# Delta stage of a decoder block: the 16x16 block inversion cut into five pieces in VectorE's queue, the decay scans given four slots

## The reference, cut to what matters

```
S = S * exp(g_t)
v_eff = (v_t - k_t S) * beta_t
S = S + k_t^T v_eff
o_t = q_t S
```

## Time and profile before

| | us |
|---|---|
| median of 3 runs | 1939.47 |
| lowest, highest run | 1939.33, 1945.62 |
| the profiled execution, its own time | 1945.92 |
| its span (first to last instruction) | 1944.0 |
| outside the span | 1.9 |

### The profile page before, as it was taken

One profiled execution on the slowest core, in us unless ns is written; L12 is line 12 of the kernel. 1 busy time (PEld: TensorE's weight loads), 2 busy tenths in 40 slices (PEclk: granted clock), 3 DMA queues, 4 the chain that ended last, 5 costly groups with the idle time before them and its releaser, 6 DMA issues. The chain is left out here.

```text
span 1944.0 us, 31429 instructions
## 1 busy us (share of the span) xinstructions
PE 1594.6 (82%) x10849; PEld 1132.2 (58%) x10849; DVE 1147.0 (59%) x2425; ACT 820.8 (42%) x1745; POOL 597.3 (31%) x547
## 2 busy tenths in 40 slices
PE   5898972379999999857589999999747999999980
PEld 3444442368888878743247776676634666666650
DVE  4898993355676666423235677777753554554545
ACT  3777771024444434423345555555312333333324
POOL 0222224222233330010023355454542333333330
PEclk9898985678899888978699999999868999999995
DMA  2232325434334543203611222310321111111117
GB/s 85 85 140 86 141 86 151 131 88 132 102 92 136 134 121 91 61 21 123 208 51 40 92 72 67 116 34 23 135 94 31 45 47 47 45 47 48 44 39 262
DMA packets 180536, 174.48 MB, mean 90 GB/s; under 512 B 87352, under 2 KB 139116, under 8 KB 180268
## 3 DMA queue, kind: packets, MB, share of 16 engines
q1 hardware_dynamic: 165771, 145.49, 24.0%
q0 software_dynamic: 10400, 22.95, 3.6%
q10 hardware_dynamic: 4224, 4.19, 0.6%
HBM read 112.54 MB, written 60.04 MB: 89 GB/s over the span
## 5 line engine op out<-in xcount | busy, mean ns | idle before, releaser
L520 DVE SCALAR_TENSOR_TENSOR conv_y<-conv_in,taps,conv_y 128x512 f32<-128x512 f32 x192 | 165.3, 875 | 19.2 <-ACT conv_y L391 14.7
L2204 POOL DMA_INDIRECT y<-o,idx x71 | 83.4, 1175 | 242.0 <-DVE o L2347 234.0
L2283 ACT ACTIVATE xsT<-pX 128x256 f32<-128x256 f32 x71 | 27.3, 384 | 303.3 <-PE pX L2228 303.3
L1647 PE MATMUL xQ<-late,last 128*128 128x512 f32 x256 | 127.2, 620 | 16.5 <-ACT late L1803 7.8
L2239 PE MATMUL pG<-w_gu,xsT 128*128 x284 | 135.5, 600 | 1.2 <-issue 0.6
L2260 PE MATMUL pD<-late,hT 128*128 x568 | 134.2, 379 | 0.0
L2239 PE MATMUL pU<-w_gu,xsT 128*128 x284 | 134.1, 594 | 0.0
L316 PE MATMUL ps_j<-xnT,w_qkv 128*128 128x512 f32 x256 | 131.2, 649 | 0.0
L1613 POOL TENSOR_TENSOR sc<-sc,den 128x1232 f32<-128x1232 f32 x32 | 72.0, 2249 | 174.6 <-DVE den L2029 174.5
L2260 PEld LDWEIGHTS pD<-late,hT 128*128 128x128 f32 x568 | 102.5, 190 | 11.0
L2343 DVE TENSOR_TENSOR o<-pD,late 128x256 f32<-128x256 f32 x71 | 30.1, 424 | 121.1 <-PE pD L2260 121.1
(11 more groups left out here) (316 smaller groups left out, 3818.6 us busy)
## 6 DMA issues: line engine op xcount, KB each, us to landing
qkvg<-tok SPq DMA_DIRECT2D x8, 2048.0 KB, 6.6
qkvg<-gate SPq DMA_DIRECT2D x8, 1024.0 KB, 8.8
step<-step SPq DMA_DIRECT2D x32, 256.0 KB, 5.5
qk<-qkvg SPq DMA_DIRECT2D x32, 256.0 KB, 6.9
vb<-qkvg SPq DMA_DIRECT2D x32, 256.0 KB
gt<-qkvg SPq DMA_DIRECT2D x32, 256.0 KB
y<-y SPq DMA_DIRECT2D x16, 512.0 KB
xin<-in_x SPq DMA_DIRECT2D x11, 512.0 KB, 4.0
```

Source lines behind the costliest of these rows:

```text
L520: y = nc.vector.scalar_tensor_tensor(conv_y[m % 4][:], conv_in[b][:, m, k:k + BT], taps[:, m, k:k + 1], conv_y[m % 4][:], ALU.mult, ALU.add)
L1647: mm = pe.matmul(Q[:], w_q[:, c, j * P:(j + 1) * P], x1T[:, c, :], start=c == 0, stop=c == KD - 1)
L2204: nc.gpsimd.indirect_dma_start(out=s["y"].rearrange("t p d -> (t p) d"), out_offset=bass.IndirectOffsetOnAxis(ap=idx[j % 8][:, 0:1], axis= ...
```

## The change

`run` gets a fourth function, `rest`, which it calls last in each slot, behind the tails. Only DVE passes one. The four scans go from `new` in slots 3 and 5 (two each) to `rest` in slots 2, 3, 4 and 5 (one each). The inversion is cut into pieces, also in `rest`: `first_blocks` in slot 9, merges 2 and 4 in slot 10, the first half of merge 8 (`upper_left`) in slot 11, its second half (`lower_right`) and `last_blocks` in slot 12. The arithmetic and the number of instructions are the same; the other engines' queues are unchanged. The core of the diff:

```diff
-        def run(new, ready, tail):
+        def run(new, ready, tail, rest=None):
...
                             tail((f - 4 * b) % SLOTS, n, n % 2, b)
+                    if rest and 0 <= c + 2 < CHUNKS:
+                        rest(f, c + 2)
...
-            def merged_blocks(m):
...
+            def upper_left(m):
+                n, w, v, wide = block_views(m)
+                link(each(v, m, corner(X16, m, 0, 0), corner(N16, m, 0, 1)))
+                link(nc.vector.tensor_reduce(W16[:, 0:w], V16[:, 0:w * m].rearrange("p (w j) -> p w j", j=m), AX_X,
+                                             ALU.add))
+
+            def lower_right(m):
+                n, w, v, wide = block_views(m)
+                link(each(v, m, wide, corner(X16, m, 1, 1)))
                 link(nc.vector.tensor_reduce(corner(X16, m, 0, 1), v, AX_X, ALU.add, negate=True))
...
             def new(f, c, par):
-                if f in (3, 5):
-                    for b in (FIRST, SECOND)[f // 5]:
-                        decays(c, b)
                 if f == 6:
...
+            def rest(f, c):
+                if f in (2, 3, 4, 5):
+                    decays(c, f - 2)
+                if f == 9:
+                    first_blocks(c)
                 if f == 10:
-                    first_blocks(c)
-                    merged_blocks(2)
-                    merged_blocks(4)
+                    for m in (2, 4):
+                        upper_left(m)
+                        lower_right(m)
                 if f == 11:
-                    merged_blocks(8)
+                    upper_left(8)
+                if f == 12:
+                    lower_right(8)
                     last_blocks()
...
-            run(new, ready, tail)
+            run(new, ready, tail, rest)
```

More of the change, by code:

```diff
@@ L1086, in first_blocks, with block_views, each @@
                 link(nc.vector.tensor_tensor(X16[:, 0:LANE], X16[:, 0:LANE], con[:, C_L1:C_L1 + LANE], ALU.add))
-            def merged_blocks(m):
+            def block_views(m):
                 n = B0 // (2 * m)
-                shape, w = [P, m, m, m], n * m * m
+                w = n * m * m
                 v = V16[:, 0:w * m].rearrange("p (n i k j) -> p n i k j", n=n, i=m, k=m)
[L1092 to L1101, removed]
+                return n, w, v, W16[:, 0:w].rearrange("p (n i k) -> p n i k", n=n, i=m)
+            def each(v, m, left, right):
+                shape = [P, m, m, m]
+                for q in range(B0 // (2 * m)):
+                    last = nc.vector.tensor_tensor(
+                        v[:, q], left[:, q].unsqueeze(2).broadcast_to(shape),
+                        right[:, q].rearrange("p j k -> p k j").unsqueeze(1).broadcast_to(shape), ALU.mult)
+                return last
+            def upper_left(m):
+                n, w, v, wide = block_views(m)
+                link(each(v, m, corner(X16, m, 0, 0), corner(N16, m, 0, 1)))
                 link(nc.vector.tensor_reduce(W16[:, 0:w], V16[:, 0:w * m].rearrange("p (w j) -> p w j", j=m), AX_X,
                                              ALU.add))
-                link(each(wide, corner(X16, m, 1, 1)))
+            def lower_right(m):
+                n, w, v, wide = block_views(m)
+                link(each(v, m, wide, corner(X16, m, 1, 1)))
                 link(nc.vector.tensor_reduce(corner(X16, m, 0, 1), v, AX_X, ALU.add, negate=True))
```

## The result

| | before | changed |
|---|---|---|
| median of 7 runs, us | 1942.26 (1938.01 to 1947.89) | 1955.79 (1938.91 to 1961.17) |
| ratio, 95% interval | | 1.0058 (1.0033 to 1.0083) |
| profiled execution, us (span) | 1945.92 (1944.0) | 1953.18 (1951.3) |

The changed kernel is slower by 0.6%, some 11 us; 1941 was forecast, and the measured median lies above the range's 1951. Repeated beside the experiments it gave 1.0046 (1.0026 to 1.0066). The loss lies in the delta stage: DVE's last statistics of it come at 864.3 us of the span before and at 870.8 after, and what follows takes 1079.7 and 1080.5 us. Of the 7.3 us between these two spans 3.6 are not the change but luck of the clock.

The account below looks back on a forecast made before the run. PE was taken to set the pace, busy 53.9 of about 58 us a step. Terms 0.8 + 6 x 0.04 + 1.8 - 1.2 = +1.6 us, added to the median 1939.47, gave 1941; range 1933 to 1951.

Parts of the forecast that it names:

- the scans' half: DVE's slots 2 to 6: the instruction list is the same before and after, so spreading the scans does nothing by itself.
- ACT, not the inversion, holds the gating of b2: Gating of b2: ACT's root is late by itself, so PE's 2.39 us stall stays; DVE's shift there +0.04 us a step.
- the +0.8 forecast: Step -1: the Y round falls behind the wait for N, moving z6 copies and `base_done` back +0.8 us, once.
- 4.5: `base_done` moves 4.5 us later in the step, and the DMAs behind it on SP shift by as much.
- The term of the scans: PE's stall on the Z round shrinks as POOL waits for loads: -0.2 us a step, -1.2 us in six.
- the y6 wait at 0.3 us a step: y6 on PE waits for the first z6 copy: 0.3 us a step, bounds 0.2 and 0.5, +1.8 us in six.
- the late loads at nothing: SP's loads behind `base_done` shift by 4.5 us, but b1's keys still land before PE wants them: cost 0.
- steady machine: Stages of a full step: about 58 us each, PE busy 53.9 of them and setting the pace.
- a margin of 1.5 us: Keys of b1: landing 9.77 us behind T's issue, from step 0, leaves 1.5 us where it was 5.6.
- Rival B: Loads land over 11.3 us behind T's issue; PE waits at L839 in five steps: 7.5 to 15 us slower, chance 0.15.
- Rival A: The low clock stretch behind PE's stall shrinks by luck of position: up to 15.4 us faster, chance 0.18 in all.
- Full and part: Low clock shrinking in all six steps, -15.4 us, chance 0.05; in one to three, -2.6 to -7.7 us, chance 0.13.

Follow-up runs that it names:

- e1: Kernel before with only the four scans moved to their new slots, the inversion left in `new`: ratio 1.0006 (0.9989 to 1.0024).
- e5: Changed kernel with the next chunk's scores loads of batches 0 to 2 issued ahead of the inverses, against the kernel before: ratio 0.9932.
- e8: Kernel before with the scores loads of batches 0 to 2 issued ahead of the inverses, DVE's queue untouched: ratio 0.9900 (0.9874 to 0.9925).
- e11: The kernel of e5 again, on the chip of e10, against the kernel before: ratio 0.9950 (0.9933 to 0.9968).
- e10: Changed kernel with `lower_right(8)` and `last_blocks` behind the z6 copies and the loads early as in e5, against the kernel before: ratio 0.9882.
- e4: Kernel before with SP sending the inverses only after DVE's z6 copies, DVE's queue untouched: ratio 1.0042 (1.0028 to 1.0057).
- e2: Kernel before with only merge 8's second half and `last_blocks` moved behind the targets of b3: ratio 1.0051 (1.0031 to 1.0072).

## Why the prediction was wrong

Right, by its own steps: the scans' half does nothing. ACT, not the inversion, holds the gating of b2, and the stall stays 2.39 us in six steps. In step -1 the time from the first use of N to the z6 copies grew from 7.77 us (395.45 to 403.22) to 8.58 (394.59 to 403.17), +0.81 for the +0.8 forecast. `base_done` moved by 4.4 us for 4.5. N was in use 3.05 us after its issue (619.10 to 622.15), the very figure of the earlier trace rows; `first_blocks` waited 0.71 us for it and PE lost nothing. The term of the scans had the right sign: PE's waits on Z in front of L841 are 2.5 us in four steps where they were 4.6 in five, for the 1.2 us forecast, though two of the four are still 0.95 us.

The step that failed is the one that put the y6 wait at 0.3 us a step and the late loads at nothing. Together they were +1.8 us in the sum. In the changed kernel's trace they are 3.6 us at y6 and a wait of 2.52 us for keys with a low clock behind it, and the change as a whole costs 9 to 11 us. Both were sized in a long step, and the kernel doesn't only have long steps. The "steady machine" of the first paragraph was one execution; e1 shows the same queue at 54.35 us a step.

- The wait at y6. From gating to the copies DVE's work has a fixed length (4.03 us). PE's work in between, the transposes and updates b3, is shorter at full clock (L933 1.16 us in place of 1.91). So the half clock hid four fifths of the wait: 0.30 us at half, 1.38 at full. With the loads early, e5 lies 0.3% above e8, and e11 lies 0.5% above e8 and 0.7% above e10.
- The loads. I had a margin of 1.5 us: landing 9.77 us behind T's issue, need 11.3 us behind it. In the step with the wait PE was ready for the keys 8.8 us behind T's issue (481.41 against 472.64), 2.5 us too early for my figure, since the stretch before ran at full clock from y6 on. And the keys were in use only at 11.29 us, 1.5 us later than in step 0. Both together make the 2.52. So the landing time, taken from one step, was too short as well: e1 shows a wait that ended 11.95 us behind T's issue (641.76 to 653.71). The wait gives the gain of the short stretch back: the step with the 2.52 us took 61.04 us, and in the repeated run a step of 54.79 us was followed by one of 63.00, with waits of 0.42 and 1.19 us and a low clock behind them. e4 shows that lateness alone costs 0.42%.

Rival B had the loads with their point of decision, at 0.15 and at 7.5 to 15 us. The measured 11 us lies in its span, but by luck in part: it was priced as 1.5 to 3 us in each of five long steps, and the trace has one wait of 2.52 us, behind a short stretch. Rival A saw that the low stretch can shrink and counted it as luck for the changed kernel; it was a state that the kernel before had already (three short steps in a row in e1), and in the two traces of the changed kernel it shows once. Full and part had 0.18 with the sign for the change reversed.

What isn't settled: why a given execution enters the short steps at all, and how the 11 us divide. That the late last piece is the cause is shown by e2. Its two effects don't add: e2 holds both and costs 0.5%, e4, the loads alone with 3.8 of the 4.4 us, costs 0.4%, and the y6 wait with the loads early costs 0.3 to 0.5%. A reason may be that each wait both delays PE and is followed by a low clock, as at 485 to 491 us, and that either of them is enough to end the short steps; this was not tested.

## What to carry to other kernels

Size a new wait at both clock levels and in the shortest step that the kernel can have, not in the one profiled: a slow stretch hides waits and late loads that appear when it ends. Before a piece is moved back in a queue, list what is issued behind its signal; here the DMAs for the next round stood behind the inverses without need, and moving them forward was worth 1.0% by itself, twice what the change lost. Look first in the start-up for such a gain: most of this one was ahead of step 1, where PE had waited 28.5 us at one place, and not in the steps that repeat. And where an engine waits for B, ask first who B waits for: a stall put down to DVE was ACT's, and giving PE other work in front of it brought, with the loads, 2.65%.

## What was not expected of the hardware

The same queue ran with a granted clock of 1.00 or of 0.91 through whole steps of the same execution (e1), 54.35 against 58.31 us, with the same 2.39 us stall in both: the stall doesn't always bring the clock down. A spread of 1938 to 1951 us over 25 runs of one kernel on one core went along with a mean clock of 0.900 to 0.891.
